# Layer one's bias row copied into the PSUM banks by ScalarE and VectorE in a fused graph and mixture-of-experts kernel

## The chip, the cores and the metric

The kernel runs on one core of one Trainium2 chip. The metric is the time of one execution on the device in microseconds (us). The core has five engines with an instruction stream each: TensorE (PE; PEld are its weight loads), VectorE (DVE), ScalarE (ACT), GpSimd (POOL) and SyncE (SP), and 16 DMA engines that all queues share. The engines wait for each other through semaphores. Matmul results go to PSUM, eight banks of 128 partitions x 512 f32.

## The reference

```python
x = x + gnn(layernorm(x), adj, ...)          # x: 2048 x 512, adj: 2048 x 2048
x_flat = layernorm(x)                        # the rows that the experts see
probs = softmax(x_flat @ Wr + br)            # 16 experts
topk_w, topk_idx = top_k(probs, 2)
h = einsum('nc,ech->neh', x_flat, W1) + b1   # layer one, 512 -> 512
h = layernorm(h) * g1 + be1
h = gelu(h)
expert_out = einsum('neh,eho->neo', h, W2) + b2
x = x + sum over the two chosen experts of topk_w * expert_out
```

The graph stage quantizes its inputs and multiplies by the adjacency matrix. The kernel computes an expert only for the rows that chose it.

## The kernel before

**Two stages.** Up to about 200 us the kernel runs the graph stage and the router; adjacency tiles stream in, and TensorE multiplies them by the quantized support. Meanwhile VectorE and GpSimd build a table of which rows go to which expert. Then follows the expert stage: the rows are cut into *slots* of 128 rows of one expert each. The plan (which slot is whose, and where an expert begins) is data: every engine reads it word by word from `plan` into registers (`load_plan`, L488), and loops over pairs of slots, an even and an odd one (`pe_pair`, `act_pair`, `dve_pair`, `pool_pair`). How many pairs there are is data as well. An "early" tile of the first expert and the first slots are computed ahead of the loop, in the transition from about 200 to 223 us.

**A slot.** Its 128 rows are gathered from DRAM (GpSimd, L747), transposed (`rows_t`, L1746), and rounded into a high part by ScalarE (`slot_x_hi`) and a low part by VectorE (`slot_x_lo`). Layer one is 12 matmuls of 128x128 by 128x512 (L1836, L1840, L1844): high rows by high weights, low rows by high weights, high rows by low weights. Then come statistics on VectorE (`slot_stats`), a reciprocal root on GpSimd (`slot_rstd`, L758), `h_hat` on VectorE (L1471), four transposes (`hidden_t`, L1860), Gelu and the high part on ScalarE, the low part on VectorE (`slot_g_lo`), layer two in 12 matmuls, a scaled copy out (`gated`) and a scatter that adds the rows into the output (GpSimd, L774). In its slot s TensorE does `hidden_t(s)`, `rows_t(s+3)`, `layer_2(s-1)` and `layer_1(s+2)`.

**The banks.** Layer one's result is in one of two PSUM banks, by the slot's parity (`h_ps`), layer two's in two others (`y_ps`). The bias of layer two is copied into the bank by ScalarE (`slot_seed`, L1032) before the matmuls add to it. The bias of layer one is a 13th matmul: `bias_product` (L1689) multiplies 128 rows of which two are one by a tile whose first two rows are the bias row's high and low part. These parts are made once on VectorE (`split_bias`), stored to DRAM and loaded expert by expert, 2 rows of 512.

**Weights.** SyncE loads an expert's bias and its weights (two halves of 512 KB a layer, `load_layer`) when the buffer of the expert before last is free. When an expert begins, ScalarE makes the high part of the next expert's weights (`split_next`, L1007) and VectorE the low part in two halves (`split_next`, L1463).

**Order.** Each engine's order is written by hand. VectorE's slot s was `h_hat(s+1)`, `g_lo(s)`, layer two's split, `x_lo(s+3)`, statistics of s+2, layer one's split. GpSimd's turn for a slot is `rstd`, a gather, a scatter; a scatter waits for earlier ones (`give`).

Of the kernel before, what the change touches and what calls it, by code (L numbers as in the profile page):

```python
# [30 lines left out]
P = 128  # L31
N = 2048
D = 512
# [42 lines left out]
def biased_in(t):  # L76
# [21 lines left out]
BIAS_OUT_IN, BIAS_IN = 6, 8  # L98
# [8 lines left out]
           ("iota_e", TOP * TQ * E), ("token_1", T), ("two_rows", 1), ("dump_row_1", 1), ("plan_mask", 5 * (E + 1)),  # L107
# [12 lines left out]
def constants():  # L120
# [31 lines left out]
    put("two_rows", (p < 2)[:, None])  # L152
# [33 lines left out]
def gnn_moe_program(nc, x, adj_steps, gnn_w, scalars, wr, br, w1, b1, g1, be1, w2, b2, consts, xn_rows, bias_dram, out):  # L186
    with ExitStack() as ctx:
# [22 lines left out]
        bias_hi = place("bias_hi", [P, D], F32R)  # L210
        bias_lo = place("bias_lo", [P, D], F32R)
        two_rows = place("two_rows", [P, P], F32R)
# [63 lines left out]
        b_raw = place("b_raw", [P, D], F32)  # L276
        end_gnn = where[0]
        bias_row1 = place("bias_row1", [P, 4 * D], F32R)
        bias_rows2 = place("bias_rows2", [P, 4 * D], F32)
# [6 lines left out]
        where[0] = end_gnn - D * 4  # L286
        e_g = place("e_g", [P, D], F32)
        e_y = e_g[:, :]
# [92 lines left out]
        bias_in = sem("bias_in")  # L381
        bias_ok = sem("bias_ok")
        bias_out = sem("bias_out")
# [30 lines left out]
        rows_ok = sem("rows_ok")  # L414
# [11 lines left out]
        y_seeded = sem("y_seeded")  # L426
        scattered = [sem(f"scattered{i}") for i in range(2)]
# [3 lines left out]
        bias_zero = sem("bias_zero")  # L431
# [37 lines left out]
        e_x_ps, e_h_ps, e_h_t_ps, e_y_ps = ps[:, 6, :], ps[:, 4, :], ps[:, 1, :], ps[:, 5, :]  # L469
        e_x_hi, e_x_lo = bias_hi, bias_lo  # L470
        e_g_hi, e_g_lo = bias_hi, bias_lo
        words_ps = ps[:, 3, 0:3 * TAB]
# [5 lines left out]
        def h_ps(par):  # L478
            return ps[:, 4 - par, :]
# [25 lines left out]
        def _(sp):  # L505
# [40 lines left out]
            def load_layer(n, e, at, par, ring):  # L546
                load_bias(n, e, at, ring)
                for h in range(2):
                    load_half(n, h, at, par)
# [28 lines left out]
            for n in range(2, STEPS + WINDOWS):  # L578
# [5 lines left out]
                if w == BIAS_OUT_IN:  # L584
                    store_biases()
# [1371 lines left out]
```

## Time and profile before

| | us |
|---|---|
| median of 3 runs | 499.54 |
| lowest and highest of them | 494.15 and 502.11 |
| the profiled execution | 495.48 |
| its span, first to last instruction | 493.7 |

| engine | busy us | share of the span |
|---|---|---|
| TensorE, matmuls | 454.7 | 92% |
| VectorE | 348.3 | 71% |
| ScalarE | 306.1 | 62% |
| GpSimd | 227.2 | 46% |

A busy time counts instructions that compute; register work, branches and semaphores are not in it. Matmuls overlap, so the time of one in its row is longer than the distance to the next. The chain that ended last is followed back from the last instruction: at each step to what released it, or to the instruction before it on its engine.

### The profile page before, as it was taken

Reading aid. Unit: us, or ns where it says so; the run is one execution under the profiler, and the core shown is the slowest. Engines: PE = TensorE matmul, PEld = TensorE weight load, DVE = VectorE, ACT = ScalarE, POOL = GpSimd, SP = SyncE. Lnnn points to the kernel's source line nnn. Section 1 sums busy time; section 2 is a strip of 40 time slices with the busy share of each in tenths; the row PEclk is TensorE's granted clock in tenths of the full one; section 3 lists DMA queues with packets and bytes.
Section 4 is the critical chain, followed back from the end, with each engine's and each line's share of the span. In section 5 each row is a group of like instructions: output and inputs, shape, how many; then the busy total and the mean of one; then the engine's idle time right before and its main releaser. Section 6 shows DMA issues by size and latency. Waiting matters only on the chain.

```text
span 493.7 us, 10242 instructions
## 1 busy us (share of the span) xinstructions
PE 454.7 (92%) x2260; PEld 374.7 (76%) x2261; DVE 348.3 (71%) x735; ACT 306.1 (62%) x511; POOL 227.2 (46%) x267
## 2 busy tenths in 40 slices
PE   0799999999999999988998999999998899999990
PEld 0478888877888888877777888888787787887870
DVE  5798864787788877876657786677878686667620
ACT  1666462474544334446777878779878885887560
POOL 3353330342155637553455555554635436455532
PEclk9999999999999999899999999999999999999997
DMA  8621224884645644239959687968789889675443
GB/s 295 272 70 58 87 64 171 292 314 172 225 156 175 208 138 135 91 105 308 288 133 253 195 250 186 260 133 218 227 257 289 262 216 288 130 191 87 86 67 42
DMA packets 33532, 91.30 MB, mean 185 GB/s; under 512 B 6160, under 2 KB 6304, under 8 KB 32992
## 3 DMA queue, kind: packets, MB, share of 16 engines
q1 hardware_dynamic: 19664, 60.60, 37.3%
q0 software_dynamic: 9232, 21.98, 21.4%
q10 hardware_dynamic: 4608, 8.39, 4.6%
q8 instruction: 11, 0.18, 0.1%
q14 instruction: 17, 0.14, 0.1%
HBM read 71.89 MB, written 19.07 MB: 184 GB/s over the span
## 4 chain that ended last, share of the span: by engine, by line
PE 62%; DMA 13%; DVE 9%; issue 6%; DVEq 2%; POOL 2%; ACT 2%; POOLq 1%; ACTq 0%; SPq 0%
PE ps L1585 17%; DMA out<-y_sb,scat_i 8%; PE ps L1836 7%; PE ps L1844 7%; PE ps L1840 7%; PE ps L1569 6%; PE ps L1557 5%; PE ps L1625 2%; DMA xg<-xn_rows,tok_i 2%; PE ps L1746 2%; PE ps L1860 2%; DVE w_split L1463 2%; PE ps L1616 1%; DMA gw_raw<-in_gnn_w 1%; PE ps L1689 1%
## 5 line engine op out<-in xcount | busy, mean ns | idle before, releaser
L774 POOL DMA_INDIRECT out<-y_sb,scat_i x35 | 60.5, 1728 | 40.6 <-DMA out<-y_sb,scat_i 29.5
L747 POOL DMA_INDIRECT xg<-xn_rows,tok_i x40 | 48.0, 1201 | 58.3 <-ACT gate L972 48.5
L1463 DVE TENSOR_TENSOR w_split<-w_raw,w_split x56 | 66.0, 1220 | 11.7 <-issue 8.5
L1021 ACT ACTIVATE g_sb<-ps,be_sb,g_sb 128x128 f32<-128x128 f32 x152 | 57.1, 456 | 17.0 <-PE ps L1860 16.7
L832 ACT ACTIVATE adj_hi<-adj_raw,small 128x1024 fp32r<-128x1024 f32 x32 | 36.8, 1150 | 40.6 <-PE ps L1585 34.7
L1471 DVE TENSOR_SCALAR h_hat<-ps,h_mv,h_rs 128x512 f32<-128x512 f32 x38 | 30.7, 808 | 43.5 <-issue 24.5
L1007 ACT ACTIVATE w_split<-w_raw x28 | 53.0, 1912 | 7.7 <-DMA w_raw<-in_w 6.4
L1153 DVE SCALAR_TENSOR_TENSOR adj_lo<-adj_raw,small,adj_hi 128x1024 fp32r<-128x1024 f32 x32 | 40.8, 1275 | 19.7 <-ACT adj_hi L832 19.6
L1585 PE MATMUL ps<-sup,adj_lo 128*128 128x512 f32 x192 | 49.2, 398 | 0.0
L1585 PE MATMUL ps<-sup,adj_hi 128*128 128x512 f32 x192 | 49.2, 398 | 0.0
L1836 PE MATMUL ps<-w_split,gt_hi 128*128 x152 | 44.6, 415 | 0.0
L658 POOL TENSOR_SCALAR rstd<-mv 128x1 f32<-128x1 f32 x15 | 13.7, 914 | 66.7 <-DVE mv L1193 66.7
L1844 PE MATMUL ps<-w_split,gt_hi 128*128 x152 | 41.0, 391 | 0.0
L1840 PE MATMUL ps<-w_split,gt_lo 128*128 x152 | 41.0, 391 | 0.0
L1585 PEld LDWEIGHTS ps<-sup,adj_lo 128*128 128x128 f32 x192 | 34.9, 188 | 6.9
L1585 PEld LDWEIGHTS ps<-sup,adj_hi 128*128 128x128 f32 x192 | 34.9, 188 | 6.8
L1836 PE MATMUL ps<-w_split,xt_hi 128*128 x148 | 40.0, 392 | 0.0
L1844 PE MATMUL ps<-w_split,xt_hi 128*128 x148 | 39.7, 390 | 0.0
L1840 PE MATMUL ps<-w_split,xt_lo 128*128 x148 | 39.6, 389 | 0.0
L758 POOL TENSOR_TENSOR h_rs<-h_rs,k_sb 128x1 f32<-128x1 f32 x38 | 25.5, 672 | 27.7 <-DVE h_rs L1399 27.4
L1000 ACT ACTIVATE y_sb<-ps,gate 128x512 f32<-128x512 f32 x38 | 26.1, 686 | 17.1 <-PE ps L1844 14.3
L1396 DVE BATCH_NORM_STATS2 h_stats<-ps 128x6 f32<-128x512 f32 x38 | 26.2, 691 | 12.7 <-PE ps L1844 12.5
(216 smaller groups left out, 955.1 us busy)
## 6 DMA issues: line engine op xcount, KB each, us to landing
w_raw<-in_w SPq DMA_DIRECT2D x64, 512.0 KB
adj_raw<-in_adj_steps SPq DMA_DIRECT2D x32, 512.0 KB, 3.5
out<-x_sb ACTq DMA_DIRECT2D x16, 256.0 KB, 2.9
xn_rows<-xn ACTq DMA_DIRECT2D x16, 256.0 KB, 2.6
bias_rows<-in_b SPq DMA_DIRECT2D x16, 256.0 KB
x_sb<-in_x SPq DMA_DIRECT2D x3, 1024.0 KB, 12.5
gw_raw<-in_gnn_w SPq DMA_DIRECT2D x1, 1024.0 KB, 5.3
x_sb<-in_x SPq DMA_DIRECT2D x2, 512.0 KB, 7.0
```

The costliest lines, as they stand in the source:

```text
L747: return pool.indirect_dma_start(to, None, xn_rows, bass.IndirectOffsetOnAxis(ap=tok_i[:, s:s + 1], axis=0)).then_inc(landed[s % 2], 16)
L774: pool.indirect_dma_start(out, bass.IndirectOffsetOnAxis(ap=at, axis=0), y_sb[:, par, :], None, compute_op=ALU.add).then_inc(scattered[par ...
L832: act.activation(adj_hi[:, par, :], adj_raw[:, par, :], ACT.Copy, scale=small[:, 0:1]).then_inc(adj_hi_ok, 1)
L1007: act.activation(w_parts(n, 0, e + 1), w_raw[:, n, :, :].rearrange("p a n -> p (a n)")[:, at], ACT.Copy).then_inc(split_hi[n], 1)
L1021: ins = act.activation(g_sb[:, par, c * P:(c + 1) * P], ht_ps(par)[:, c * P:(c + 1) * P], ACT.Gelu, scale=g1_sb[:, bass.ds(e * C + c, 1)], ...
L1153: dve.scalar_tensor_tensor(adj_lo[:, par, :], adj_raw[:, par, :], small[:, 0:1], adj_hi[:, par, :].bitcast(F32), ALU.mult, ALU.subtract).t ...
L1463: ins = dve.tensor_tensor(w_parts(n, 1, e + 1, 2 * h, 2), w_raw[:, n, :, :].rearrange("p a n -> p (a n)")[:, at], w_parts(n, 0, e + 1, 2 * ...
L1471: dve.tensor_scalar(h_hat[:, par, :], h_ps(par), h_mv[:, par, 0:1], h_rs[:, par, 0:1], ALU.subtract, ALU.mult).then_inc(h_hat_ok, 1)
L1585: ins = pe.matmul(acc_bank(t), part[:, n % 2, k * P:(k + 1) * P], sup[:, first_k + k, :], start=first_k + k == 0 and not half, stop=first_ ...
L1836: pe.matmul(dst, act_hi[:, par, c * P:(c + 1) * P], w_part(n, 0, e, c), start=False, stop=False, skip_group_check=n == 1)
L1840: pe.matmul(dst, act_lo[:, par, c * P:(c + 1) * P], w_part(n, 0, e, c), start=False, stop=False, skip_group_check=n == 1)
L1844: ins = pe.matmul(dst, act_hi[:, par, c * P:(c + 1) * P], w_part(n, 1, e, c), start=False, stop=c == C - 1, skip_group_check=n == 1)
```

## The change

The bias product goes. Layer one's bias rows lie in DRAM as 128 equal rows (as layer two's did) and are loaded as such, 128 x 512, into `bias_rows[0]`. Ahead of a slot's layer one, its bank is filled by a copy: ScalarE fills the bank of even slots, late in its odd slot, and VectorE that of odd slots, in its even slot behind `g_lo`. `layer` then waits for the copy. `clear_h`, one matmul, readies VectorE's bank once. The early tile and the first slot are filled by ScalarE too (`early_seed`); the early tile's layer two now uses the bank of its layer one, so its fill comes behind `early_h_hat`. Slot 0 has its layer one in bank 5. `split_bias`, the DRAM copy of its parts and two fills on GpSimd go.

VectorE's slot begins with `g_lo`. It ends with half of layer one's split, `h_hat` of the slot ahead, and the other half (`split_around_h_hat`).

```diff
-            def load_bias(n, e, at, ring):
-                if n:
-                    sp.dma_start(bias_rows2[:, ring], b2[at, :]).then_inc(raw_in[1], 16)
-                else:
-                    sp.dma_start(bias_row1[0:2, ring].bitcast(F32), bias_dram[e]).then_inc(raw_in[0], 16)
+            def load_bias(n, at, ring):
+                sp.dma_start(bias_rows[n][:, ring], (b1, b2)[n][at, :]).then_inc(raw_in[n], 16)
...
             norm_xn(T - 2)
             store_xn(T - 2)
             gate_exp(3)
+            act.wait_ge(acc_read, T - 1)
+            early_seed(e_h_ps, 0, 0)
             finish_t(T - 2)
+            act.wait_ge(acc_read, T)
+            early_seed(h_ps(0, 0), 0, 1)
             act.wait_ge(small_in, 64)
             act.wait_ge(last_xn_ok, 1)
             store_xn(T - 1)
             finish_t(T - 1)
-            early_seed()
             early_h_hat()
             slot_x_hi(0, 0)
             slot_gate(0, 0, 1)
             gate_exp(4)
+            act.wait_ge(e_h_hat_ok, 1)
+            early_seed(e_y_ps, 1, 0)
             act.preload_act_table(ACT.Gelu)
             early_gelu()
...
+            def slot_h_seed(s, e, freed):
+
+                act.wait_ge(raw_in[0], e * 48 + 48)
+                act.wait_ge(h_hat_ok, freed)
+                act.activation(h_ps(s, 0), bias_rows[0][:, bass.ds((e & 3) * D, D)], ACT.Copy).then_inc(h_seeded[0], 1)
...
                 gated(s - 1, 1 - par, landed)
+                if par and not last:
+                    slot_h_seed(s + 3, expert_in(word, par + 3), s + 2)
...
             slot_seed(0, 0, expert_in(word, 0))
+            act.wait_ge(e_y_ok, 1)
+            slot_h_seed(2, expert_in(word, 2), 1)
             slot_gelu(0, 0, expert_in(word, 0))
...
+            def split_around_h_hat(s, par, e, start):
+
+                with dve.If(start == 1):
+                    dve.wait_ge(split_hi[0], e + 2)
+                    split_half(0, e, 0)
+                slot_h_hat(s, par)
+                with dve.If(start == 1):
+                    split_half(0, e, 1).then_inc(split_lo[0], 1)
...
+            def slot_h_seed(s, e, freed):
+
+                dve.wait_ge(raw_in[0], e * 48 + 48)
+                if freed is not None:
+                    dve.wait_ge(h_hat_ok, freed)
+                dve.tensor_copy(h_ps(s, 1), bias_rows[0][:, bass.ds((e & 3) * D, D)]).then_inc(h_seeded[1], 1)
...
             def slot(s, par, word, earlier):
 
-                slot_h_hat(s + 1, 1 - par)
                 slot_g_lo(s, par)
+                if not par:
+                    slot_h_seed(s + 3, expert_in(word, par + 3), s + 2)
                 split_next(1, expert_in(earlier, 1 - par), starts_in(earlier, 1 - par))
                 slot_x_lo(s + 3, 1 - par)
                 slot_stats(s + 2, par)
-                split_next(0, expert_in(word, par + 2), starts_in(word, par + 2))
+                split_around_h_hat(s + 2, par, expert_in(word, par + 2), starts_in(word, par + 2))
...
-            def bias_product(dst, row):
-
-                pe.matmul(dst, two_rows[:, :], bias_row1[:, row], start=True, stop=False)
+            def clear_h():
+
+                pe.matmul(h_ps(1, 1), ident_r[:, :], tab_rows[:, :], start=True, stop=True).then_inc(h_cleared, 1)
...
                 pe.wait_ge(split_hi[n], e + 1)
-                if n:
-                    pe.wait_ge(y_seeded, s + 1)
-                else:
-                    bias_product(dst, bass.ds((e & 3) * D, D))
+                pe.wait_ge(*filled)
                 pe.wait_ge(hi_ok, s + 1)
```

On TensorE, in the loop, between layer two of one slot and layer one of another, before:

```order
L1844 MATMUL ps<-w_split,gt_hi 128x512
L1829 REGISTER_ALU x3
L1689 REGISTER_ALU
L1689 ISA
L1689 MATMUL ps<-bias_row_112,two_rows 128x512
L1834 REGISTER_ALU
L1836 REGISTER_ALU
L1836 ISA
L1836 MATMUL ps<-w_split,xt_hi 128x512
```

And the same place in the changed kernel:

```order
L1841 MATMUL ps<-w_split,gt_hi 128x512
L1829 REGISTER_ALU x3
L1830 REGISTER_ALU
L1831 REGISTER_ALU
L1833 REGISTER_ALU
L1833 ISA
L1833 MATMUL ps<-w_split,xt_hi 128x512
```

The matmul at L1689 is gone; the register work of L1830 is for the wait on the copy.

On VectorE, at the end of the last pair of the loop, before (L1459 is the branch around a split, L1518 to L1520 the loops' edges; `h_rs` is the input of the reciprocal root):

```order
L1399 TENSOR_SCALAR h_rs<-h_mv 128x1
...
L1463 TENSOR_TENSOR w_split<-w_raw,w_split 128x1024
L1463 ISA x2
L1463 TENSOR_TENSOR w_split<-w_raw,w_split 128x1024
L1459 UNCONDITIONAL_BRANCH
L1520 REGISTER_ALU
L1520 COMPARE_AND_BRANCH
...
L1471 TENSOR_SCALAR h_hat<-ps,h_mv,h_rs 128x512
L1475 REGISTER_ALU
L1476 TENSOR_TENSOR gt_lo<-g_sb,gt_hi 128x512
```

And now:

```order
L1379 TENSOR_SCALAR h_rs<-h_mv 128x1
...
L1440 TENSOR_TENSOR w_split<-w_raw,w_split 128x1024
L1453 UNCONDITIONAL_BRANCH
L1463 TENSOR_SCALAR h_hat<-ps,h_mv,h_rs 128x512
L1457 COMPARE_AND_BRANCH
L1440 REGISTER_ALU x2
L1440 ISA x2
L1440 TENSOR_TENSOR w_split<-w_raw,w_split 128x1024
L1457 UNCONDITIONAL_BRANCH
...
L1475 TENSOR_TENSOR gt_lo<-g_sb,gt_hi 128x512
```

`h_hat` now stands between the halves and ahead of the loops' edges, with one branch more; inside the loop the two plan words are also read behind it.

On ScalarE, in the odd slot, in the changed kernel (`bias_rows_111` is layer one's):

```order
L979 ACTIVATE y_sb<-ps,gate 128x512
L1015 ISA
L1016 REGISTER_ALU
L1017 REGISTER_ALU
L1017 ISA
L1017 ACTIVATE ps<-bias_rows_111 128x512
L983 REGISTER_ALU x2
L983 COMPARE_AND_BRANCH
```

The rows from L1015 to L1017 are new: the copy stands between the scaled copy out and the splits.

## Rows read from the trace of the kernel before

**Rows 1.** The page: span, and busy time of each engine.
```profile
span 493.7 us, 10242 instructions
...
PE 454.7 (92%) x2260; PEld 374.7 (76%) x2261; DVE 348.3 (71%) x735; ACT 306.1 (62%) x511; POOL 227.2 (46%) x267
```

**Rows 2.** The page: the chain that ended last, by engine.
```profile
PE 62%; DMA 13%; DVE 9%; issue 6%; DVEq 2%; POOL 2%; ACT 2%; POOLq 1%; ACTq 0%; SPq 0%
```

**Rows 3.** Stretches: length, busy PE, PEld, DVE, ACT, POOL, clock, DMA share, GB/s.
```profile
261.00:347.00 86.00, 85.76 (x429) 71.54 (x429) 61.37 (x99) 70.32 (x127) 45.53 (x39) 1.00 0.79 210
347.00:411.00 64.00, 60.32 (x297) 49.30 (x297) 47.77 (x72) 51.82 (x92) 30.42 (x27) 1.00 0.89 264
```

**Rows 4.** Bias products (ns min/median/max); the chain, 261 to 345 us: start, us.
```profile
L1689 PE MATMUL ps<-bias_row,two_rows x39: 389/389/775, 200.3 to 468.7; 128*128 x37, 128*128 128x512 f32 x2
...
264.81 0.23 PE ps L1689
```

**Rows 5.** The chain elsewhere: start us, us, what.
```profile
208.79 0.43 PE ps L1689
...
223.38 0.37 PE ps L1689
...
361.97 8.48 DMA out<-y_sb,scat_i
...
392.10 5.67 DMA out<-y_sb,scat_i
...
415.12 0.23 PE ps L1689
...
468.84 0.23 PE ps L1689
```

**Rows 6.** Copies of one size, ScalarE by line, VectorE in order of time.
```profile
L1032 ACT ACTIVATE ps<-bias_rows x38: 578/598/607, 222.6 to 476.2; 128x512 f32 x38
...
104.15 0.42 DVE L1203 CAST bias_hi<-b_raw 128x512 fp32r<-128x512 f32 x1
104.60 0.69 DVE L1204 TENSOR_TENSOR bias_lo<-b_raw,bias_hi 128x512 fp32r<-128x512 f32 x1
```

**Rows 7.** Waits (us in total, times, longest): 261 to 347 us, then 347 to 411.
```profile
DVE h_hat L1471 <- issue: 9.0, 4, 2.4
...
DVE h_stats L1396 <- PE ps L1844: 6.6, 6, 2.5
...
ACT w_split L1007 <- DMA w_raw<-in_w: 6.4, 3, 3.4
```

**Rows 8.** The transition: a stretch of 4 us, and ScalarE's table copy.
```profile
208.00:212.00 4.00, 4.00 (x18) 3.40 (x17) 1.95 (x11) 3.13 (x6) 2.46 (x6) 0.70 0.70 225
...
212.87 0.60 ACT L991 ACTIVATE tab_rows<-ps 128x512 fp32r<-128x512 f32 x1 [1.70 <-PE ps L1652]
```

**Rows 9.** VectorE in order of time at two of TensorE's waits; idle before in brackets.
```profile
257.80 2.36 DVE L1463 TENSOR_TENSOR w_split<-w_raw,w_split  x2 [0.72 <-issue]
260.08 0.80 DVE L1471 TENSOR_SCALAR h_hat<-ps,h_mv,h_rs 128x512 f32<-128x512 f32 x1
...
450.94 0.81 DVE L1471 TENSOR_SCALAR h_hat<-ps,h_mv,h_rs 128x512 f32<-128x512 f32 x1 [2.32 <-issue]
```

**Rows 10.** TensorE in order of time: its waits for a gather and at h_hat.
```profile
235.39 0.66 PE L1746 MATMUL ps<-k_sb,xg 128*128 128x128 f32 x4 [1.80 <-DMA xg<-xn_rows,tok_i]
...
260.93 0.66 PE L1860 MATMUL ps<-k_sb,h_hat 128*128 128x128 f32 x4 [1.56 <-DVE h_hat L1471]
...
390.37 0.66 PE L1860 MATMUL ps<-k_sb,h_hat 128*128 128x128 f32 x4 [1.31 <-DVE h_hat L1471]
...
451.81 0.66 PE L1860 MATMUL ps<-k_sb,h_hat 128*128 128x128 f32 x4 [0.43 <-DVE h_hat L1471]
```

**Rows 11.** DMA issues, KB each.
```profile
bias_rows<-in_b SPq DMA_DIRECT2D x16, 256.0 KB
...
bias_row<-bias_dram SPq DMA_DIRECT2D x16, 4.0 KB
```

More of the change, by code:

```diff
@@ L97 @@
 GATED = BATCHES[0:3] + ((11, 5),)
-BIAS_OUT_IN, BIAS_IN = 6, 8
+BIAS_IN = 8
 LN_EPS = 1e-5
@@ L275, in gnn_moe_program @@
         xn_t = place("xn_t", [P, 2, D], F32)
-        b_raw = place("b_raw", [P, D], F32)
+        e_g = place("e_g", [P, D], F32)
+        e_y = e_g[:, :]
         end_gnn = where[0]
-        bias_row1 = place("bias_row1", [P, 4 * D], F32R)
-        bias_rows2 = place("bias_rows2", [P, 4 * D], F32)
+        bias_rows = [place(f"bias_rows{n}", [P, 4 * D], F32) for n in (1, 2)]
         e_xg = place("e_xg", [P, ROW], F32)
@@ L426, in gnn_moe_program @@
         y_seeded = sem("y_seeded")
+        h_cleared = sem("h_cleared")
+        h_seeded = [sem(f"h_seeded{i}") for i in range(2)]
         scattered = [sem(f"scattered{i}") for i in range(2)]
@@ L468, in gnn_moe_program, with h_ps @@
         compact_ps = ps[:, 7, 0:TAB]
[L469 to L472, printed above, removed]
+        e_x_ps, e_h_ps, e_h_t_ps, e_y_ps = ps[:, 6, :], ps[:, 4, :], ps[:, 1, :], ps[:, 4, :]
+        e_x_hi, e_x_lo = early_hi_sb, early_lo_sb
+        e_g_hi, e_g_lo = early_hi_sb, early_lo_sb
+        words_ps = ps[:, 2, 0:3 * TAB]
         def xt_ps(par):
             return ps[:, par, :]
-        def h_ps(par):
-            return ps[:, 4 - par, :]
+        def h_ps(s, par):
+            return ps[:, 5 if isinstance(s, int) and s == 0 else 4 - par, :]
         def ht_ps(par):
@@ L1491, in _ @@
             rest = dve.value_load(pairs[0:1, 0:1], min_val=E // 2 - 2, max_val=SLOTS // 2 - 2)
+            dve.wait_ge(h_cleared, 1)
+            slot_h_seed(1, expert_in(word, 1), None)
             early_lo(1, 1, 0)
@@ L1698, in early_part @@
                     ins = pe.matmul(dst, act_part[:, c * P:(c + 1) * P], w_part(n, low, 0, c),
-                                    start=False, stop=last and c == C - 1, skip_group_check=n == 1)
+                                    start=False, stop=last and c == C - 1, skip_group_check=True)
                 return ins
@@ L1751, in first_part @@
                 for c in range(C):
-                    ins = pe.matmul(h_ps(0), act_part[:, 0, c * P:(c + 1) * P], w_part(0, low, 1, c),
-                                    start=False, stop=last and c == C - 1)
+                    ins = pe.matmul(h_ps(0, 0), act_part[:, 0, c * P:(c + 1) * P], w_part(0, low, 1, c),
+                                    start=False, stop=last and c == C - 1, skip_group_check=True)
                 return ins
@@ L1861, in hidden_t, with slot @@
                 ins.then_inc(h_tp, 1)
-            def slot(s, par, e_before, e_ahead, landed):
+            def slot(s, par, e_before, e_ahead, landed, pair):
                 hidden_t(s, par)
```

116 lines of the change are left out of this document (42 added, 74 removed).

## The prediction, made before the change was run

> **What bounds the kernel now.** I read the page first. The span is 493.7 us and TensorE is busy for 92% of it [rows 1], but a share over the whole span mixes stages, so the second view is the chain that ended last. It gives TensorE 62% and the DMA engines 13% [rows 2]. The reader should see there that both of the things that this change touches, a TensorE instruction and DMA traffic, can lie on the path, each in some stretches. The third view splits the expert loop (about 223 to 476 us) by stretch [rows 3]. From 261 to 347 us TensorE is busy for 85.76 of 86 us: it alone is the limit. From 347 to 411 us the DMA engines are 89% busy at 264 GB/s and TensorE pauses. In the first of these the chain is TensorE and nothing else [rows 4]; in the second it runs through scatters of 6 to 9 us [rows 5].
>
> The bias product that the change removes lasts 0.39 us in its own row, but matmuls overlap: on the chain it takes 0.23 us, the distance to the matmul behind it [rows 4]. That is its price, not the row's. One slot takes 2 times 12 such products, 8 transposes and this one.
>
> **The change part by part.**
>
> *The bias products go.* There are 39. What counts is how many lie on the chain. I counted its pieces at L1689: two ahead of the loop proper, 0.43 us (at half clock) and 0.37 us; 13 from 261 to 345 us, 0.23 us each, of which the first is shown [rows 4]; five behind 411 us, of which the first and last are shown [rows 5]. Sum: 0.80 + 13 x 0.23 + 5 x 0.23 = 4.9 us. None lies on the chain from 347 to 411 us, where scatters and weight loads set the end, so I give that stretch no gain.
>
> *The copies that take their place.* ScalarE's copy of a bias row into PSUM is in the trace: 0.60 us [rows 6]. There is no such copy on VectorE. Its bounds are the two rows of the same 128x512 size: 0.42 us for a one-input copy within SBUF and 0.69 us for an operation of two inputs [rows 6]. I take 0.60, ScalarE's price for the same thing, which lies between. The Trainium skill ("VectorE: DVE Perf Modes", "What auto-detection actually checks") says that the mode with two elements per clock needs source and destination in SBUF for f32 data, which a copy into PSUM does not have, so it speaks for the dear end; no row here shows the copy. By the page the price would be 0.69 and the sum below would be the same, with the chance of the second rival a little higher.
> Each engine makes one copy in two slots. TensorE needs a bank about a slot after the copy is queued, so the copy is not itself on the path; what it costs is VectorE's and ScalarE's time. From 261 to 347 us VectorE waits 6.6 us in all for TensorE at the statistics [rows 7]. It loses 13 x 0.23 = 3.0 us of that (TensorE comes sooner) and spends 6.5 copies x 0.60 = 3.9 us: together 6.9, just the 6.6 that it has. What gives it room is the moved h_hat, next. Behind VectorE's copy stand g_lo's followers, the split of layer two, x_lo and the statistics; behind ScalarE's the two splits' first halves. I take 0 for the copies (range 0 to 3 us).
> In the transition ScalarE's copy for the early tile's layer two moves behind h_hat, 0.6 us into what was busy time. It delays the Gelu by that much; TensorE comes for its result later, and ScalarE itself stands idle for 1.70 us before the table copy behind it [rows 8]. Cost 0; 0.6 if that cover is gone. The one matmul of `clear_h`, 0.23 us, stands where TensorE waits for the first gathers: 0.
>
> *h_hat moves.* Before, VectorE ends a slot with both halves of a split (1.2 us each), at the end of a pair also steps its loop and loads two plan words, and only then makes h_hat, for which TensorE waits. Now only half a split stands ahead of h_hat and the loop's edge stands behind it. The edge shows as "issue": VectorE was idle for 2.32 us ahead of the h_hat at 450.94 us and waited for nothing [rows 9]; in the stretch from 261 to 347 us such gaps are 9.0 us [rows 7]. TensorE's waits at h_hat are these [rows 10]: 1.56 us at 260.93, where h_hat stood right behind a split of 2.36 us [rows 9]. Half a split earlier, h_hat would end at 259.8 and TensorE start 1.08 us sooner. 1.31 us at 390.37, also behind a split; but the chain there runs through a scatter at 392.10 us [rows 5], so I count nothing. 0.43 us at 451.81, behind a loop edge: gone. Sum: 1.08 + 0.43 = 1.5 us. The second half of a split comes 0.8 us later than before; TensorE needs it a slot later, which hides that.
>
> *More DMA.* Each layer-one bias load was 4 KB and becomes 256 KB, on the queue ahead of the two weight halves [rows 11]; 16 loads are 4 MB. At 264 GB/s [rows 3] one takes 0.95 us. If DMA set the pace throughout 347 to 411 us, its five loads would cost 4.8 us; if they fit into gaps, nothing. ScalarE waited for a weight load three times there, 6.4 us in all [rows 7], two of the waits long. I charge these two: 1.9 us. In the transition TensorE waits 1.80 us for a gather [rows 10] that shares the engines with the first such load: 0 to 0.95, I take 0.5. The loads beside the adjacency stream lie under TensorE's matmuls: 0. The work that goes (GpSimd's two fills, VectorE's three bias operations, two stores) stood beside a busy TensorE: 0.
>
> **Sum.** TensorE's granted clock is 0.70 from 208 to 212 us [rows 8], after its waits for the last tiles: for part of that stretch it had its lower level, 1.2 GHz, hence the 0.43 us above. Whether the dip stays, moves or goes is worth about 1.5 us (3 us of matmuls at half speed) either way; I take 0 and keep it in the range. -4.9 - 1.5 + 1.9 + 0.5 = -4.0 us. The profiled execution took 495.48 us (span 493.7 and 1.8 around it), so its changed form would take 491.5. That execution is among the fast ones: the three other times are 494.15, 499.54 and 502.11. The mean of all four is 497.8 and I put the forecast there: 497.8 - 4.0 = 493.8 us.
>
> **The rivals.**
> 1. *Everything keeps up.* All 39 products are gained (39 x 0.23 = 9.0) and the waits at 260.93, 390.37 and 451.81 give 1.08 + 1.07 + 0.43 (the second by the same half split), with the loads hidden: -11.6, so 486.2 us. For it: ScalarE and VectorE are idle for a fifth to three tenths of both stretches [rows 3]. Against it: the chain of scatters, which the change doesn't touch, sets 347 to 411 us.
> 2. *The loop becomes VectorE's or ScalarE's.* The copies' 6.9 us against 6.6 [rows 7] decide; if the loop edge still blocks VectorE (it now waits for rstd at h_hat instead of passing the time with the edge), TensorE's 4.9 us become waits at h_hat, while the 1.5, the 1.9 and the 0.5 stay: +0.9, so 498.7 us.
> 3. *Slower: weight loads.* If ScalarE had to wait for each of the 14 layer-one loads issued in the loop, each 0.95 us later, nothing of TensorE's time would be gained there: 14 x 0.95 - 0.80 = +12.5, so 510.3 us. It decides where a load takes longer than an expert's slots, as in the three waits of 347 to 411 us; from 261 to 347 us ScalarE never waited for a load ahead of a split, which speaks against it. The Trainium skill ("DMA: Bandwidth & Descriptors", "Queues, rings and completion order") says that each DMA engine serves the queues in turn by packet; by that the added packets would also lengthen gathers and scatters, which speaks for this rival. By that rule the price has no upper end of its own; no row here shows the effect apart from others.
>
> **How the numbers follow.** Forecast (TensorE-bound stretches gain, the dense stretch gives part back) 0.54: 493.8 us, its own range 489 to 498. Rival 1: 0.22. Rival 2: 0.17. Rival 3: 0.07. The three times of before spread over 8 us, which widens every case by some 3 us. From 485.0 to 502.0 us lie the forecast, most of the first rival and nearly all of the second; outside stay rival 3 and the low half of the spread around 486.2. A measurement of this kernel can tell about 2%, 10 us, from no change: below 487.8 us is faster, above 507.8 slower. Faster: most of rival 1 and the forecast's tail, 0.18. Slower: most of rival 3, 0.06. Within: 0.76.
>
> **What would show it.** A slot from 270 to 340 us takes 6.35 us from one h_hat transpose to the next, instead of 6.58: the first term. VectorE's idle time at h_hat is put down to GpSimd's rstd, and no longer to "issue"; the wait at 260.93 is down to half a microsecond and the one at 451.81 is gone: the second. VectorE's copy is between 0.42 and 0.69 us and its wait for TensorE at the statistics is near nothing, but not turned into waits of TensorE: the third. ScalarE's waits for weights between 347 and 411 us are longer by some 1 us each: the fourth. What would make the prediction wrong: TensorE waiting for a seeded bank, which I hold to be early by most of a slot; ScalarE's copy delaying its splits, so that weights come free later and loads start later; or waits at h_hat in the stretch that had none.

## The result, and the profile after

The changed kernel is slower by about 0.8%. Its median is 499.24 us (18 runs, 495.36 to 502.93); the kernel before, measured beside it, has 494.63 us (18 runs, 490.92 to 502.11). The ratio is 1.0078, 95% interval [1.0052, 1.0105]. I had forecast a gain of 4.0 us; the loss is 4.6 us by the medians and 3.9 us by the ratio. The forecast itself, 493.8 us, stood on a mean of four times of before that was 3 us too high (497.8), which hides part of the miss: by its own terms it was wrong by about 8 us. That 499.24 lies between the stated 485.0 and 502.0 us owes more to that base and to the width than to the reasoning.

The page after, its span, busy times and the chain that ended last by engine and by line:

```profile
span 497.3 us, 10396 instructions
...
PE 449.3 (90%) x2222; PEld 367.1 (74%) x2223; DVE 359.1 (72%) x751; ACT 314.1 (63%) x532; POOL 222.2 (45%) x264
...
PE 42%; DMA 17%; DVE 12%; issue 11%; ACT 5%; DVEq 5%; POOL 3%; SPq 2%; POOLq 1%; ACTq 1%
PE ps L1587 15%; DMA w_raw<-in_w 8%; PE ps L1559 6%; PE ps L1571 6%; DMA out<-y_sb,scat_i 5%; DVE w_split L1440 4%; PE ps L1837 3%; PE ps L1841 3%; PE ps L1833 3%; PE ps L1627 2%; PE ps L1547 1%; DVEq L1440 1%; DVE h_stats L1376 1%; DMA adj_raw<-in_adj_steps 1%; DVEq L480 1%
```

TensorE is busy for 5.4 us less than before [rows 1], as is to be expected without 39 products. The span is 3.6 us longer all the same, so TensorE is idle for 9.0 us more. It has lost a third of its share of the chain (62% before [rows 2]), and VectorE and the weight loads (`w_raw`) have gained.

Where in the program this happens is read from the distance between the transposes of `h_hat`, one group in each slot. In the kernel before, some of them were (start us, us, engine, line, operation; idle time before in brackets):

```profile
222.73 0.65 PE L1860 MATMUL ps<-k_sb,h_hat 128*128 128x128 f32 x4 [0.65 <-issue]
...
239.05 0.60 PE L1860 MATMUL ps<-k_sb,h_hat 128*128 128x128 f32 x4
...
340.03 0.60 PE L1860 MATMUL ps<-k_sb,h_hat 128*128 128x128 f32 x4
...
471.64 0.60 PE L1860 MATMUL ps<-k_sb,h_hat 128*128 128x128 f32 x4
```

The same slots after (the 1st, 3rd, 4th, 18th, 19th, 22nd, 23rd, 27th and 37th of 38):

```profile
221.78 0.65 PE L1857 MATMUL ps<-k_sb,h_hat 128*128 128x128 f32 x4 [0.65 <-issue]
...
239.93 0.60 PE L1857 MATMUL ps<-k_sb,h_hat 128*128 128x128 f32 x4
246.26 0.60 PE L1857 MATMUL ps<-k_sb,h_hat 128*128 128x128 f32 x4
...
336.67 0.60 PE L1857 MATMUL ps<-k_sb,h_hat 128*128 128x128 f32 x4
346.29 0.65 PE L1857 MATMUL ps<-k_sb,h_hat 128*128 128x128 f32 x4 [1.46 <-issue]
...
365.37 0.66 PE L1857 MATMUL ps<-k_sb,h_hat 128*128 128x128 f32 x4
375.61 0.65 PE L1857 MATMUL ps<-k_sb,h_hat 128*128 128x128 f32 x4 [1.67 <-issue]
...
404.93 0.65 PE L1857 MATMUL ps<-k_sb,h_hat 128*128 128x128 f32 x4 [0.18 <-issue]
...
474.30 0.60 PE L1857 MATMUL ps<-k_sb,h_hat 128*128 128x128 f32 x4
```

| stretch | before | after | difference |
|---|---|---|---|
| up to the 1st transpose | 222.73 | 221.78 | -0.95 |
| 1st to 3rd | 16.32 | 18.15 | +1.83 |
| 3rd to 18th (15 slots) | 100.98 | 96.74 | **-4.24** |
| 18th to 37th (19 slots) | 131.61 | 137.63 | **+6.02** |
| 37th to the end | 22.1 | 23.0 | +0.9 |

An undisturbed slot takes 6.33 us (239.93 to 246.26). So the gain is there, and from the 3rd to the 18th transpose most of it is kept: 15 slots that are some 0.25 us shorter and the wait of 1.56 us at 260.93 [rows 10], less two new waits at `h_hat` (0.92 us at 291.67 and 0.31 us at 330.22). Behind that, where most experts have two slots, it is lost one and a half times over. Three slots are each more than 2 us longer than the same slot before: 336.67 to 346.29 (9.62 us, 7.32 before), 365.37 to 375.61 (10.24 us, 8.10 before) and 396.26 to 404.93 (8.67 us, 6.58 before). What TensorE waits for, from 228 to 480 us (us in total, times, longest):

```profile
PE ps L1857 <- DVE h_hat L1463: 5.4, 8, 1.7
PE ps L1857 <- issue: 3.3, 3, 1.7
PE ps L1745 <- DMA xg<-xn_rows,tok_i: 3.0, 2, 2.3
PE ps L1841 <- DVE w_split L1440: 1.9, 2, 1.4
PE ps L1833 <- ACT gt_hi L1005: 1.2, 1, 1.2
PE ps L1837 <- DVE gt_lo L1475: 1.0, 3, 0.6
```

These are 15.8 us (0.9 us more are in two shorter rows). Before there were only waits ahead of the transposes (5.1 us for `h_hat` and 1.9 us put down to `issue`) and for the gather (1.8 us). The new ones are for VectorE's splits and `gt_lo`, and one for ScalarE's `gt_hi`. TensorE never waits for a filled bank here: the copies are in time, so what they cost has to be looked for in other work of the two engines. VectorE around the slot of 9.62 us:

```profile
336.63 0.69 DVE L1475 TENSOR_TENSOR gt_lo<-g_sb,gt_hi 128x512 fp32r<-128x512 f32 x1 [1.53 <-issue]
337.24 0.69 DVE L1471 COPY ps<-bias_rows 128x512 f32 x1
...
338.43 0.69 DVE L1376 BATCH_NORM_STATS2 h_stats<-ps 128x6 f32<-128x512 f32 x1
...
340.41 1.23 DVE L1440 TENSOR_TENSOR w_split<-w_raw,w_split  x1 [0.77 <-issue]
341.55 0.81 DVE L1463 TENSOR_SCALAR h_hat<-ps,h_mv,h_rs 128x512 f32<-128x512 f32 x1
342.27 1.22 DVE L1440 TENSOR_TENSOR w_split<-w_raw,w_split  x1
343.40 0.69 DVE L1475 TENSOR_TENSOR gt_lo<-g_sb,gt_hi 128x512 fp32r<-128x512 f32 x1
344.01 2.35 DVE L1440 TENSOR_TENSOR w_split<-w_raw,w_split  x2
```

and the matmul that waits for it, here and in two kernels of the experiments below, x1 (no copies on VectorE) and x2 (no loop copies on ScalarE):

```profile
343.63 1.20 PE L1841 MATMUL ps<-w_split,xt_hi 128*128 x4 [1.38 <-DVE w_split L1440]
...
340.64 1.20 PE L1837 MATMUL ps<-w_split,xt_hi 128*128 x4 [0.46 <-DVE w_split L1440]
...
345.51 1.17 PE L1838 MATMUL ps<-w_split,xt_hi 128*128 x4 [1.42 <-DVE w_split L1436]
```

From `gt_lo` at 336.63 on VectorE waits for no other engine that this view names. The copy stands in that row, and the split at 342.27, for which TensorE waits at 343.63, comes late. Without VectorE's copies the same wait is 0.46 us (x1), without ScalarE's it stays at 1.42 us (x2), so most of it is the copy's. The rest goes with the move of `h_hat`, which now stands ahead of that second half: in the kernels that have `h_hat` in its old place (before, x4, y5) TensorE's list of waits in the loop has none for a split.

Not everything in these slots is VectorE's time. The 1.46 us ahead of the transposes at 346.29 are no wait for `h_hat`, which ended at 342.36; they are put down to `issue`, and without any copy they are there as well (1.47 us in x0). In the slot of 10.24 us TensorE waits 1.21 us for ScalarE's `gt_hi`, and ScalarE had waited 3.17 us for weights just before.

### The profile page after: what moved, and what is told of

Its sections match the earlier page's. It is cut to its first block, busy times and chain, and to the rows that moved or that the text cites. A ratio compares the mean times of both kernels' runs of the same rounds, so it can differ in the third digit from the quotient of the medians.

```text
span 497.3 us, 10396 instructions
## 1 busy us (share of the span) xinstructions
PE 449.3 (90%) x2222; PEld 367.1 (74%) x2223; DVE 359.1 (72%) x751; ACT 314.1 (63%) x532; POOL 222.2 (45%) x264
## 4 chain that ended last, share of the span: by engine, by line
PE 42%; DMA 17%; DVE 12%; issue 11%; ACT 5%; DVEq 5%; POOL 3%; SPq 2%; POOLq 1%; ACTq 1%
PE ps L1587 15%; DMA w_raw<-in_w 8%; PE ps L1559 6%; PE ps L1571 6%; DMA out<-y_sb,scat_i 5%; DVE w_split L1440 4%; PE ps L1837 3%; PE ps L1841 3%; PE ps L1833 3%; PE ps L1627 2%; PE ps L1547 1%; DVEq L1440 1%; DVE h_stats L1376 1%; DMA adj_raw<-in_adj_steps 1%; DVEq L480 1%
## 5 line engine op out<-in xcount | busy, mean ns | idle before, releaser
L1440 DVE TENSOR_TENSOR w_split<-w_raw,w_split x56 | 67.1, 1220 | 12.8 <-issue 9.5
L749 POOL DMA_INDIRECT out<-y_sb,scat_i x35 | 61.9, 1768 | 31.7 <-DMA out<-y_sb,scat_i 17.1
L722 POOL DMA_INDIRECT xg<-xn_rows,tok_i x40 | 45.4, 1134 | 63.3 <-ACT gate L946 54.1
L1475 DVE TENSOR_TENSOR gt_lo<-g_sb,gt_hi 128x512 fp32r<-128x512 f32 x38 | 26.1, 687 | 23.8 <-issue 13.5
L1837 PE MATMUL ps<-w_split,xt_lo 128*128 x148 | 40.7, 397 | 0.2 <-DVE xt_lo L1372 0.2
L733 POOL TENSOR_TENSOR h_rs<-h_rs,k_sb 128x1 f32<-128x1 f32 x38 | 23.9, 628 | 37.9 <-DVE h_rs L1379 37.8
L1837 PEld LDWEIGHTS ps<-w_split,gt_lo 128*128 128x128 f32 x152 | 28.0, 188 | 8.6 <-DVE gt_lo L1475 2.3
```

Source lines behind the costliest of these rows:

```text
L722: return pool.indirect_dma_start(to, None, xn_rows, bass.IndirectOffsetOnAxis(ap=tok_i[:, s:s + 1], axis=0)).then_inc(landed[s % 2], 16)
L749: pool.indirect_dma_start(out, bass.IndirectOffsetOnAxis(ap=at, axis=0), y_sb[:, par, :], None, compute_op=ALU.add).then_inc(scattered[par ...
L1440: return dve.tensor_tensor(w_parts(n, 1, e + 1, 2 * h, 2), w_raw[:, n, :, :].rearrange("p a n -> p (a n)")[:, at], w_parts(n, 0, e + 1, 2 ...
L1837: pe.matmul(dst, act_lo[:, par, c * P:(c + 1) * P], w_part(n, 0, e, c), start=False, stop=False, skip_group_check=True)
```

## The experiments

The theories. **V**: VectorE has no time for its copies where experts are short. **S**: ScalarE's copy waits for VectorE's `h_hat` (12.6 us in nine waits over the whole loop, of which 3.3 us from 347 to 411), and the splits behind it come late. **D**: the 4 MB of added loads cost it. **M**: the moved `h_hat` costs it. All ratios are to the kernel before, run beside each.

| kernel | us | ratio [95%] |
|---|---|---|
| changed kernel | 499.24 | 1.0078 [1.0052, 1.0105] |
| x1: no copies on VectorE | 493.97 | 0.9952 [0.9921, 0.9982] |
| x2: no loop copies on ScalarE | 496.15 | 1.0006 [0.9973, 1.0039] |
| x0: neither | 493.39 | 0.9939 [0.9906, 0.9973] |
| x0s: neither, small loads | 489.49 | 0.9880 [0.9839, 0.9921] |
| x3: small loads | 497.34 | 1.0025 [0.9990, 1.0060] |
| x4: h_hat back | 502.90 | 1.0127 [1.0085, 1.0170] |
| y1: before, h_hat moved alone | 495.36 | 0.9995 [0.9964, 1.0025] |
| y2: ScalarE's copy earlier | 499.37 | 1.0090 [1.0056, 1.0124] |
| y3: all loop copies on ScalarE | 493.36 | 0.9948 [0.9921, 0.9976] |
| y4: VectorE's copy ahead of g_lo | 499.97 | 1.0075 [1.0047, 1.0103] |
| y5: y3 with h_hat back | 496.59 | 1.0018 [0.9986, 1.0049] |
| y6: y3, bias load behind the weights | 493.91 | 0.9965 [0.9935, 0.9995] |
| z1: one more ScalarE copy | 502.25 | 1.0158 [1.0107, 1.0209] |
| z2: one more VectorE operation | 501.94 | 1.0161 [1.0105, 1.0217] |
| z3: before, one more VectorE operation | 498.00 | 1.0059 [1.0030, 1.0088] |
| z4: changed kernel again | 499.30 | 1.0076 [1.0044, 1.0108] |

### Whose copies cost: x1, x2, x0

x1 takes VectorE's copies away, so that the tiles of odd slots lack the bias of layer one:

```diff
-                if not par:
-                    slot_h_seed(s + 3, expert_in(word, par + 3), s + 2)
                 split_next(1, expert_in(earlier, 1 - par), starts_in(earlier, 1 - par))
...
-                pe.wait_ge(*filled)
+                if filled is not None:
+                    pe.wait_ge(*filled)
...
-                    pe.matmul(dst, ..., start=False, ...
+                    pe.matmul(dst, ..., start=filled is None and c == 0, ...
```

> The changed kernel without VectorE's copies of the bias row: in odd slots the first matmul of layer one starts its bank itself, so the odd slots' tiles lack the bias of layer one. Everything else, the loads too, stays. The changed kernel took 499.2 us, the one before 494.6. Theory V (VectorE's 19 copies of 0.69 us come where it has no time, in slots that start an expert, and splits and h_hat come late): most of the loss goes, 493 us, and TensorE's waits for VectorE's h_hat and splits shrink to those of before. Theory S (ScalarE's copy waits for VectorE's h_hat, 12.6 us in 9 waits, and holds up the splits behind it): the wait gets a little shorter as VectorE is ahead, 498 us. Theory D (4 MB more of loads make weights late): 499 us. Theory M (the moved h_hat is what costs): 499 us.

It took 0.9952 of before: 1.26% below the changed kernel, 6.2 us, as V expected. x2 takes away ScalarE's copies in the same way:

> The changed kernel without ScalarE's copies in the loop: in even slots from slot 2 on the first matmul of layer one starts its bank itself, so these tiles lack the bias of layer one; VectorE's copies and the loads stay. Theory S: 9 waits of 12.6 us are gone from ScalarE and with them the late splits; 493 to 494 us, and ScalarE's waits for weight loads fall back to the 6.4 us of before. Theory V: 498 to 499 us, since VectorE has as much to do as in the changed kernel. Theories D and M: 499 us.

1.0006: a gain too, of 0.7%, between what V and S expected. x0 takes away both and leaves the loads:

> The changed kernel without any copy of layer one's bias in the loop, with the full loads of 256 KB: the layer's first matmul starts its bank, and the loop's tiles lack that bias. The same with small loads was 0.988 of before. Theory D: the loads cost here what they cost among the copies, 0.5%: 0.993. Theory that ScalarE's copies cost 0.7% on their own, apart from VectorE's: 0.988 (0.9952 without VectorE's copies, less 0.7%). If ScalarE's copies cost only where VectorE is late too: 0.994 to 0.995, what it is with ScalarE's copies and without VectorE's.

0.9939. So without VectorE's copies, ScalarE's cost 0.1% (x1 against x0), within the error; beside them, 0.7%. VectorE's cost 0.7% alone (x2 against x0) and 1.3% beside ScalarE's. Together they cost 1.4%, 6.9 us, where the forecast had 0. TensorE's waits at `h_hat` and for VectorE's splits in x0, from 228 to 480 us, are 3.8 us where the changed kernel has 7.3:

```profile
PE ps L1849 <- DVE h_hat L1459: 2.5, 3, 1.4
...
PE ps L1833 <- DVE w_split L1436: 1.3, 3, 0.5
```

### Place or time: y2, y4, y3

y2 undoes what S blames. ScalarE's copy moves to where the `h_hat` that it waits for has been read already, and no split stands right behind it:

```diff
                 slot_seed(s, par, e_s)
+                if not par and not last:
+                    slot_h_seed(s + 2, expert_in(word, par + 2), s + 1)
                 slot_gelu(s, par, e_s)
...
-                if par and not last:
-                    slot_h_seed(s + 3, expert_in(word, par + 3), s + 2)
```

> The changed kernel with ScalarE's copy for the bank of even slots moved from late in the odd slot to the next slot's start, behind the copy of layer two's bias: by then TensorE has already read the h_hat that the copy waits for, and no split stands right behind the copy. Theory S: the wait of 12.6 us goes and the splits come as they did before; 1.001 of before, as without these copies at all. Theory that the 0.6 us of ScalarE's time is what costs, wherever it stands: 1.006 to 1.008, as in the changed kernel, since Gelu now stands behind the copy.

1.0090: no gain. In the trace ScalarE's wait for `h_hat` at this copy falls from 12.6 to 2.1 us, and the time stays: S in this form falls. y4 puts VectorE's copy ahead of `g_lo`:

```diff
-                slot_g_lo(s, par)
                 if not par:
                     slot_h_seed(s + 3, expert_in(word, par + 3), s + 2)
+                slot_g_lo(s, par)
```

> The changed kernel with VectorE's copy ahead of g_lo instead of behind it: it then runs while VectorE would wait for ScalarE's gt_hi (10.3 us in all at g_lo), and in slots that start an expert it stands in the row as before. Theory V as a matter of sheer time in the slots that start an expert: no change, 1.006 to 1.009 of before. Theory that the order is at fault (the copy queued behind a wait that it doesn't need): 1.000 or less.

1.0075: no change, so this place is no better. (It has a price of its own: TensorE's waits for `gt_lo` are 3.2 us in its trace, 1.0 us in the changed kernel's.) y3 is y2 with VectorE's copies in the loop given to ScalarE, at the same place in odd slots (VectorE's lines go as in x1):

```diff
-                if not par and not last:
-                    slot_h_seed(s + 2, expert_in(word, par + 2), s + 1)
+                if not last and not isinstance(s, int):
+                    slot_h_seed(s + 2, expert_in(word, par + 2), s + 1, par)
```

> As the run before, but ScalarE makes the copies of odd slots too, each at the start of a slot, and VectorE makes none in the loop. Theory V (VectorE has no room for 17 copies of 0.69 us) with room on ScalarE, which is idle for 16% of the loop: 0.989 of before (the changed kernel's 1.0078, less 1.26% for VectorE's copies, less 0.7% for the wait). If ScalarE has no room either: 1.005 and more, with TensorE waiting for gt_hi and xt_hi.

0.9948, 1.4% below y2, with as many copies in all. The loop copies of odd slots cost 1.4% more on VectorE than on ScalarE, and with all loop copies on ScalarE they cost nothing that can be told (x0, with none, is 0.9939). y3 is the version to keep: it is faster than the kernel before by 0.5%, and than the changed one by 1.3%. TensorE now waits for ScalarE's fills (L1017) for 3.1 us, and for `h_hat` for 1.8 instead of 5.4:

```profile
PE ps L1831 <- ACT ps L1017: 3.1, 2, 1.6
PE ps L1855 <- issue: 2.4, 4, 1.5
...
PE ps L1855 <- DVE h_hat L1463: 1.8, 2, 1.5
```

### Doubling the suspects: z1, z2, z3, z4

z2 adds an operation of the same length behind VectorE's copy, z3 adds the like (between `bias_hi` and `bias_lo`) to the kernel before behind `g_lo` and nothing else, z1 adds a copy behind ScalarE's. The added lines of z2 and of z1:

```diff
+                    dve.tensor_tensor(early_lo_sb[:, :], early_hi_sb[:, :].bitcast(F32), early_hi_sb[:, :].bitcast(F32), ALU.subtract)
...
+                    act.activation(early_lo_sb[:, :], early_hi_sb[:, :].bitcast(F32), ACT.Copy)
```

> The changed kernel with VectorE's copy followed by an operation of the same length (0.69 us) whose result nobody reads, 17 times. Theory V as VectorE's sheer time: the same price again, 1.3%, 1.020 of before, and TensorE's waits for h_hat and VectorE's splits grow. Theory that the first copy's cost is its place or the order and not its time: 1.008 to 1.010.

> The kernel before with one more VectorE operation of 0.69 us in even slots, behind g_lo, whose result nobody reads; nothing else. Forecast's reading (6.6 us of waits at the statistics in 261 to 347 us are room, 6.5 operations use 4.5 of them): 1.000 of before. Theory V (VectorE has no room in the slots that start an expert, and its waits lie in the others): 1.005 to 1.013.

> The changed kernel with ScalarE's copy followed by a second one of the same size whose result nobody reads, 17 times. Theory that ScalarE's copies cost 0.7% beside VectorE's (the changed kernel without them was 1.0006): another 0.7%, 1.015 of before. Theory that ScalarE has the time and that run was low by chance: 1.008, as the changed kernel.

> The changed kernel as it is, beside the three others: 1.0078 of before. If it comes out below 1.004, the difference of 0.7% to the run without ScalarE's copies was chance.

z4 is the changed kernel once more: 1.0076. z2 is at 1.0161, 0.85% above it. That is less than the 1.3% that x1 gave for the first copy, though the two agree within their errors (some 0.6% each way for z2 and z1, of 6 runs each), and it is clear of zero. TensorE's waits for `h_hat` and for VectorE's splits are 9.7 us in its trace, 7.3 in the changed kernel's and 7.4 in z4's. z3 is the plainest of all: 0.69 us more of VectorE in every second slot make the **kernel before** slower by 0.59%, 2.9 us. The 17 operations last 11.6 us together, so a quarter of their time reaches the end: VectorE had room for most of it before the change, but not for all. z1 is at 1.0158: ScalarE's time, late in the slot and beside VectorE's copies, costs 0.8% for another 0.6 us in every second slot. That, and z4, speak against chance in x2's 0.7%.

What stays open is why ScalarE's copies are dear beside VectorE's and free without them, and why they cost the same at the early place (y2). The two engines hand work to each other (`gt_hi` to `g_lo`, the first half of a split to the second), so a late ScalarE could keep VectorE waiting, which would count only when VectorE is behind. The traces don't show it: from 228 to 480 us VectorE waited 7.1 us for `gt_hi` in the changed kernel and 0.7 us in x2, but 7.9 us in x1, which is fast.

### The loads: x3, x0s, y6

x3 loads two rows where the loop loads 128 (the copies stay):

```diff
-                load_bias(n, at, ring)
+                load_bias(n, at if n else first, ring, P if n else 2)
```

> The changed kernel with loads of two rows (4 KB) of layer one's bias where the loop's loads bring 128 rows (256 KB), so that most rows of the bias are not those of the expert; all copies stay. Theory D: the 14 loads of the loop at 0.95 us each are 13 us at most, the five of the dense stretch 4.8 us; 494 to 495 us, and the pieces of w_raw on the chain that ended last go. Theories V, S and M: 499 us, within 1.

1.0025, 0.5% below the changed kernel. (GpSimd also zeroes half of the tile once, as in the kernel before.) x0s does the same to x0:

> The changed kernel without any copy of layer one's bias in the loop and with loads of two rows: the layer's first matmul starts its bank and the loop's tiles lack that bias. It shows what the bias product, the move of h_hat and the shorter slot are worth when nothing takes their place. If the forecast's first rival priced the gain rightly: 11.6 us, 0.977 of before. If other limits (VectorE's splits, weight loads and scatters in the dense stretch) cap it: 0.985 to 0.990, with TensorE waiting in 347 to 411 us as long as before or longer.

0.9880, 0.6% below x0. Two pairs of kernels give the loads 0.5 to 0.6%, 2.6 to 2.9 us, each with an error of about 0.5%. x0s also shows what the change gives when nothing takes the product's place: 1.2%, 5.9 us. It isn't the 11.6 us of the first rival: TensorE still waits 2.7 us in all from 347 to 411 us, where it waited 3.2 us before. y6 loads the bias behind the weights and counts it apart, on top of y3:

```diff
-                load_bias(n, at, ring)
+                if n:
+                    load_bias(n, at, ring)
                 for h in range(2):
                     load_half(n, h, at, par)
+                if not n:
+                    load_bias(n, at, ring)
```

> All loop copies on ScalarE, and the load of layer one's bias behind the two weight halves, counted apart, so that a split no longer waits for it. Theory D as a matter of order (the 256 KB stand ahead of the weights that a split waits for): 0.990 of before, since small loads gave 0.5%. If it is the DMA engines' time (89% busy from 347 to 411 us before) and not the order: 0.995, as without this edit.

0.9965 against y3's 0.9948: the same. So it isn't their place ahead of the weights that costs. That leaves the DMA engines' time, which no run changed by itself.

### The move of h_hat: x4, y1, y5

x4 puts `h_hat` back into its old place in the changed kernel:

```diff
             def slot(s, par, word, earlier):
+                slot_h_hat(s + 1, 1 - par)
                 slot_g_lo(s, par)
...
-                split_around_h_hat(s + 2, par, expert_in(word, par + 2), starts_in(word, par + 2))
+                split_next(0, expert_in(word, par + 2), starts_in(word, par + 2))
```

> The changed kernel with h_hat back where it stood before: at the start of VectorE's slot, behind the whole split and the loop's edge. Theory M (with h_hat ahead of the edge VectorE waits for rstd in line, then still has the edge to do, and g_lo comes late): 496 us. Theory S: h_hat comes later and ScalarE's copy waits longer for it, by half a split or by the edge in its 9 waits; 501 to 502 us. Theories V and D: 499 to 501 us, as the move was forecast to save 1.5.

1.0127, 0.5% above the changed kernel, at the edge of the error; M falls. Most of TensorE's waits in the loop are then for `h_hat`, 14.8 us instead of the changed kernel's 5.4:

```profile
PE ps L1859 <- DVE h_hat L1463: 14.8, 11, 2.5
```

y1 makes the move alone, in the kernel before:

> The kernel before with VectorE's new order alone (half a split, h_hat, half a split, the loop's edge behind it); bias products and loads as before. By the forecast's second term 1.5 us are gained, 0.997 of before; the changed kernel with h_hat moved back was 1.0127 of before and the changed kernel 1.0078, which gives the move 2.4 us, 0.995. Theory M (the move does harm unless the copies need it): 1.000 or more.

0.9995: nothing. In its trace TensorE's waits for `h_hat` from 228 to 480 us are 1.8 us instead of 5.1, but new ones stand beside them, one of them for a split:

```profile
PE ps L1854 <- DVE w_split L1460: 1.0, 1, 1.0
```

y5 puts `h_hat` back in y3, where VectorE makes no copies in the loop:

> All loop copies on ScalarE at the start of its slots (that was 0.9948 of before), and h_hat back at the start of VectorE's slot. Theory that the moved h_hat pays because slots are now TensorE's 6.33 us and VectorE has no slack left: 1.000, as the move gave 0.5% among VectorE's copies. Theory that it pays only beside VectorE's copies (alone in the kernel before it gave nothing): 0.995.

1.0018 against 0.9948: there the move is worth 0.7%, 3.5 us. It pays where slots are shorter, with VectorE's loop copies (x4) or without them.

## Why the prediction was wrong

**The bias products: right.** Slots were to go from 6.58 to 6.35 us; they take 6.33. With the move and without copies and added loads the change brings 5.9 us (x0s), where the forecast's terms for the products and for `h_hat`, -4.9 and -1.5, made 6.4.

**The copies: this step failed.** I took 0 from a range of 0 to 3; they cost 6.9 us (the changed kernel against x0). The size of one copy was only a little off. I took 0.60 us; it is 0.69, the dear bound:

```profile
L1471 DVE COPY ps<-bias_rows 128x512 f32 x19 | 13.0, 686 | 1.3 <-issue 1.3
```

The Trainium skill ("VectorE: DVE Perf Modes", "What auto-detection actually checks") spoke for that end, and the trace agrees, at 686 ns; 19 times 0.086 us are 1.6 us. What was wrong is the room. I counted VectorE's waits for TensorE at the statistics, 6.6 us, from 261 to 347 us alone [rows 7], and set against their sum what the change takes of them there, 3.9 us of copies and 3.0 us by which TensorE comes sooner: 6.9 against 6.6.

Even in that stretch the sum told the wrong thing. VectorE still waits 2.7 us for TensorE there after the change:

```profile
DVE h_stats L1376 <- PE ps L1841: 2.7, 2, 1.7
```

These waits are the ones at 265.46 (1.67 us) and 317.28 (1.05 us). By the sum there was room left, and yet TensorE, which was idle for 0.24 us of the 86 before [rows 3], is idle for 4.07 us of them (its row stands below). TensorE's waits lie in other slots, at 291.67, 330.22, 343.63 and 346.29 us: what VectorE waits in one slot is no room in another.

And nine more copies lie behind 347 us, 9 x 0.69 = 6.2 us of VectorE's time, for which I looked up nothing. TensorE's idle time grows by another 5 us there (3.68 to 5.84 us from 347 to 411, 1.61 to 4.47 from 411 to 480). The same view of the kernel before, from 347 to 440 us, would have told:

```profile
DVE h_stats L1396 <- PE ps L1844: 0.4, 1, 0.4
```

VectorE waited for TensorE once in 93 us, for 0.4 us. It was busy for only 75% of the dense stretch [rows 3]; of the rest, 8.3 us up to 411 us were waits for rstd and 3.1 us for ScalarE's splits, which a copy behind `g_lo` doesn't fill. z3 shows the lack of room without any of the rest of the change. The Trainium skill ("Perfetto Trace Analysis", "Identifying the Most-Contended Engine") calls the occupancy of an engine like VectorE a fair measure of "how close you are to roofline". For the room for one more operation it was none here: at 71% over the span [rows 1] 0.69 us more in every second slot cost 0.59% (z3).

"ScalarE's copy delaying its splits", which I named as what would make the prediction wrong, looked like the cause in the trace; y2 took most of that wait away and gained nothing. TensorE waiting for a filled bank wasn't the cause either: there is no such wait.

**h_hat: the mechanism right, the account not.** The wait at 260.93 [rows 10] is gone. That at 451.81 is still there, with 0.48 us at 454.76. It isn't the copies' doing: x0 has it without any (0.47 us at 447.65), and y1, with the move but the longer slots, has none there. The second half of a split comes later, as the forecast said, but that was not always hidden: the waits for splits above go with it. The loop's edge left `h_hat` and now stands ahead of `g_lo`; in the whole span:

```profile
L1463 DVE TENSOR_SCALAR h_hat<-ps,h_mv,h_rs 128x512 f32<-128x512 f32 x38 | 30.7, 808 | 21.3 <-POOL h_rs L733 21.3
...
L1475 DVE TENSOR_TENSOR gt_lo<-g_sb,gt_hi 128x512 fp32r<-128x512 f32 x38 | 26.1, 687 | 23.8 <-issue 13.5 <-ACT gt_hi L1005 10.3
```

As forecast, nothing at `h_hat` is put down to "issue" any more. The term was 1.5 us: the runs give 0.2 us in the kernel before (y1, no difference that can be told), 2.4 us in the changed one (x4, at the edge of the error) and 3.5 us in y3 (y5).

**The loads: right in size, not in form.** The terms were 1.9 and 0.5 us, 2.4 together; x3 and x0s give 2.6 and 2.9 for all. (One load of 128 x 512 f32, 262144 bytes, takes 0.99 us at 264 GB/s and not 0.95; that changes the sum by 0.1 us.) ScalarE's waits for weights from 347 to 411 us were to grow by about 1 us each, from 6.4 us [rows 7]. Those ahead of the splits did not; one of 1.4 us is new, ahead of layer two's copy:

```profile
ACT w_split L986 <- DMA w_raw<-in_w: 5.8, 3, 3.2
ACT ps L1017 <- DVE h_hat L1463: 3.3, 2, 2.1
ACT ps L1011 <- DMA w_raw<-in_w: 1.4, 1, 1.4
```

The DMA share there is 87% at 267 GB/s, hardly other than before [rows 3].

```profile
261.00:347.00 86.00, 81.93 (x411) 67.73 (x410) 64.76 (x103) 71.89 (x132) 44.27 (x39) 1.00 0.80 218
347.00:411.00 64.00, 58.16 (x283) 46.67 (x282) 47.89 (x73) 51.51 (x93) 26.63 (x25) 1.00 0.87 267
```

**The clock: 0 was about right in this execution.** The dip of 208 to 212 us [rows 8] is gone, 0.30 x 4 = 1.2 us, with 0.5 us more from the 4 us ahead of it (0.88 before, 1.00 after), and another stands at 232 to 240 us (rows below), 0.05 x 4 + 0.38 x 4 = 1.7 us.

**The rivals.** The second, that the loop becomes VectorE's or ScalarE's, is nearest to what happened. Its 498.7 us are close to the measured 499.24 mostly by chance: its change was +0.9 us, on a base 3 us too high, where +3.9 was measured. It looked for the loss from 261 to 347 us, where less than half of TensorE's added idle time lies, and at `h_hat`, where the waits hardly grew (5.1 to 5.4 us); most of the new ones stand at splits, `gt_lo`, `gt_hi` and the gather and in `issue`. I gave it 0.17, because its point of decision, 6.9 us against 6.6, was worked out in the stretch with the most room.

## What to carry to other kernels

Work moved onto an engine that isn't the limit has to be set against that engine's waits in the tightest stretch that it will run in, not in the stretch where the gain is read. The share of busy time doesn't tell the room there, and neither does the sum of its waits for the engine that sets the pace: they have to lie in the slots in which the work is added. Where such waits are next to nothing, as from 347 to 440 us here, expect added work to cost. Before such a change is built, put a dummy operation of its length into the kernel as it is (z3), and where two engines can take the work, try both (y3).

## What was not expected of the hardware

TensorE's granted clock fell behind a long pause of TensorE, and as pauses moved, the dips moved. After the change, as stretches (length, busy PE, PEld, DVE, ACT, POOL, clock, DMA share, GB/s):

```profile
208.00:212.00 4.00, 3.36 (x19) 2.50 (x19) 3.35 (x15) 3.94 (x8) 3.49 (x7) 1.00 0.82 255
...
232.00:236.00 4.00, 1.64 (x10) 1.08 (x9) 2.54 (x5) 3.71 (x9) 0.55 (x1) 0.95 1.01 350
236.00:240.00 4.00, 4.00 (x13) 3.10 (x12) 2.96 (x3) 1.87 (x5) 3.22 (x2) 0.62 1.01 348
```

```profile
234.81 0.66 PE L1745 MATMUL ps<-k_sb,xg 128*128 128x128 f32 x4 [2.33 <-DMA xg<-xn_rows,tok_i]
235.50 1.99 PE L1833 MATMUL ps<-w_split,xt_hi 128*128 x4
237.28 1.89 PE L1837 MATMUL ps<-w_split,xt_lo 128*128 x4
238.99 1.10 PE L1841 MATMUL ps<-w_split,xt_hi 128*128 x4
```

After a wait of 2.33 us for a gather, eight matmuls took twice as long (1.2 GHz, the lower level) and the ninth on took the usual time; that is about 1.7 us. With 0.5 us more of waiting for the gather than before, and without two products, it makes up the 1.83 us that the table shows lost from the 1st to the 3rd transpose. In the kernel before, the wait of 1.80 us at 235.39 [rows 10] has no dip behind it. Two of x4's dips, at 392 to 400 and at 416 to 424 us, come after waits at `h_hat` of 2.27 and 2.47 us. Over many executions the mean clock of the changed kernel was 0.985 (17) and that of the kernel before 0.989 (29). Among the executions of before, a clock lower by 0.01 went with 3.2 to 5.1 us more (four sets of 22 to 35); by that, 1.2 to 2 us of the 3.9 may be TensorE's slower clock after more pauses. This is an estimate and rather too high, since pauses lengthen a run by themselves and no run changed the clock alone. Nor does the clock tell the kernels apart: y3, the fastest that is complete, has 0.985 as well. Single executions of one kernel also differ by several us, so where a difference is below 1%, the medians of a dozen runs decide and the traces only say where to look.
